# Attention part of a small conv network: full-width products as column-tile pairs, and a new instruction order

## The reference

```
layer 0: q = Wq x + bq (8 x N)   k = Wk x + bk (8 x N)   v = Wv x + bv (32 x N)
         attn = softmax(q^T k)   out = Wo (v attn^T) + bo   x1 = gamma * out + x
layer 1: same with v 64 x N and no Wo:               x2 = x1 + v attn^T
layer 2: batch norm, relu, 3x3 conv with sign weights, twice, plus shortcut
layer 3: per-channel 4x4 whitening over the whole batch (cholesky), 4x4 mix, bias
```

## Time and profile before

| | us |
|---|---|
| median of 3 runs | 70.65 (70.19 to 70.87) |
| profiled execution, its own time | 70.66 |
| its span, first to last instruction | 68.9 |

### The profile page before, as it was taken

One profiled execution on the slowest core, in us unless ns is written; L12 is line 12 of the kernel. 1 busy time (PEld: TensorE's weight loads), 2 busy tenths in 40 slices (PEclk: granted clock), 3 DMA queues, 4 the chain that ended last, 5 costly groups with the idle time before them and its releaser, 6 DMA issues.

```text
span 68.9 us, 1828 instructions
## 1 busy us (share of the span) xinstructions
PE 58.2 (85%) x654; PEld 34.6 (50%) x654; DVE 47.4 (69%) x129; ACT 43.0 (62%) x133; POOL 21.9 (32%) x59
## 2 busy tenths in 40 slices
PE   5997866839999899989695899979998999999910
PEld 2253531416364364445261457358974998774300
DVE  0029799487796987878699754677949969377440
ACT  0710498939989898989999593464008672455440
POOL 4001606860371817355303317470004050008200
PEclk9999999999999999999999999999999999999999
DMA  0889830000000000000000000000000000000025
GB/s 0 237 255 275 274 149 6 0 0 0 0 0 0 10 5 0 0 0 5 0 0 0 5 10 0 0 0 10 0 0 0 0 10 10 0 0 0 0 102 202
DMA packets 2168, 2.69 MB, mean 39 GB/s; under 512 B 368, under 2 KB 1520, under 8 KB 2160
## 3 DMA queue, kind: packets, MB, share of 16 engines
q1 hardware_dynamic: 1872, 2.39, 10.9%
q10 hardware_dynamic: 288, 0.20, 0.9%
HBM read 2.06 MB, written 0.52 MB: 37 GB/s over the span
## 4 chain that ended last, share of the span: by engine, by line
PE 54%; ACT 12%; DVE 11%; POOL 11%; issue 5%; POOLq 1%; DVEq 0%; ACTq 0%
PE bank L760 13%; PE bank L690 9%; ACT bank L458 8%; PE bank L590 6%; PE bank L600 5%; PE bank L624 4%; DVE cut L908 4%; PE bank L735 3%; PE bank L671 3%; POOL zn L405 2%; PE bank L656 2%; PE bank L661 2%; POOL cut L355 2%; POOL cut L358 2%; ACT hi L523 2%
## 5 line engine op out<-in xcount | busy, mean ns | idle before, releaser
L458 ACT ACTIVATE bank<-bank,negmax 128x256 f32<-128x256 f32 x32 | 14.3, 447 | 1.2 <-DVE negmax L898 1.0
L590 PE MATMUL bank<-const-bfloat16-1.0 128*128 128x512 bf16 x39 | 11.2, 419 | 0.8 <-PEq L1177 0.8
L898 DVE TENSOR_REDUCE negmax<-bank 128x2 f32<-128x512 f32 x16 | 10.4, 684 | 1.3 <-PE bank L640 1.3
L471 ACT ACTIVATE probs<-bank 128x512 f32<-128x512 f32 x16 | 8.6, 590 | 0.5 <-PE bank L661 0.5
L690 PE MATMUL bank<-probs,vt 128*64 128x256 f32 x64 | 8.7, 391 | 0.0
L908 DVE TENSOR_SCALAR cut<-bank,prm 128x256 f32<-128x256 f32 x8 | 3.9, 482 | 6.2 <-PE bank L600 6.1
L760 PE MATMUL bank<-hi,taps 64*64 64x225 f16 (+2 forms) x144 | 7.3, 267 | 0.8 <-ACT hi L523 0.8
L760 PE MATMUL bank<-lo,taps 64*64 64x225 f16 (+2 forms) x144 | 7.0, 265 | 0.0
L760 PEld LDWEIGHTS bank<-hi,taps 64*64 64x64 bf16 x144 | 6.0, 107 | 1.9 <-issue 0.9
L458 ACT ACTIVATION_READ_ACCUMULATOR bank<-bank,negmax 128x1 f32 x32 | 6.6, 205 | 0.0
L590 PEld LDWEIGHTS bank<-const-bfloat16-1.0 128*128 128x128 bf16 x39 | 3.9, 108 | 5.2 <-issue 2.5
(11 more groups left out here) (132 smaller groups left out, 101.6 us busy)
## 6 DMA issues: line engine op xcount, KB each, us to landing
cw<-conv_w SPq DMA_DIRECT2D x2, 288.0 KB, 4.6
x<-x_in SPq DMA_DIRECT2D x4, 128.0 KB, 2.7
out<-res SPq DMA_DIRECT2D x2, 256.0 KB, 2.1
kst<-consts SPq DMA_DIRECT2D x1, 428.0 KB, 5.6
aw<-attn_w ACTq DMA_DIRECT2D x1, 128.0 KB, 2.4
aw<-attn_w SPq DMA_DIRECT2D x1, 128.0 KB, 3.2
half<-select SPq DMA_DIRECT2D x1, 96.0 KB, 2.7
kst<-consts SPq DMA_DIRECT2D x1, 64.5 KB, 2.9
```

The costliest lines, as they stand in the source:

```text
L458: nc.scalar.activation(part, part, ACT.Exp, bias=negmax[:, i % 2, n:n + 1], accum_out=total[:, i % 2, n:n + 1]).then_inc(total_out, 1)
L471: nc.scalar.activation(probs[:, i % 2, g], pb_t[g][:].rearrange("p (t n) -> p t n", t=CH), ACT.Exp).then_inc(exp_out, 1)
L590: mm(bank[:], filler, filled, start=True, stop=True)
L898: ve.tensor_reduce(negmax[:, i % 2, g * CH:(g + 1) * CH], pb_s[(2 * i + g) % 3][:].rearrange("p (t n) -> p t n", t=CH), AX.X, ALU.max, neg ...
```

## The change

Three things. First, in the attention part every product with 128 outputs is issued as two with 64 outputs each (column tiles 0 to 63 and 64 to 127): project, replicate, values, shifts_to_rows, the fillers and the identity product of item 7. The products of batch norm and whitening stay as they are; `value_weights` stays too. Second, the order of all four engines' programs is written out call by call instead of in loops. `scores_t(i)` is split into the score products and `add_shifts(i)`; `totals` can be issued by halves, with its Ln as `logs(i)`; `later_parts` of POOL becomes `parts1` and `parts2`. shifts(0) no longer has to follow the later parts of item 1 by its wait, but stands behind those of items 1 and 2 by order; those of item 3 follow it. Signs stay behind the last exps, as they were; weight_sum(1) goes to the end of the attention part, weight_sum(0) and both power_of_two to its late middle. Third, some banks move: `pb_e` to bank 0 (so value_weights waits for qk_out of item 2 and replicate(3) for const0), `proj(3)` to `pb_v`. Fillers: (6, 1, 2) at the start become (6, 1, 5, 4), the two near the end go.

```diff
-WARM_START = (6, 1, 2)
-WARM_ATTENTION = (1, 1, 4, 2)
+WARM_START = (6, 1, 5, 4)
-        pb_e = banks[5]
+        pb_e = banks[0]
-            return (banks[7] if i in (1, 3) else pb_pv)[:, N:2 * N]
+            return {1: banks[7], 3: pb_v}.get(i, pb_pv)[:, N:2 * N]
...
 keep_warm
-                    mm(bank[:], filler, filled, start=True, stop=True)
+                    for h in range(2):
+                        mm(bank[lanes(h)], filler[:, lanes(h)], filled, start=True, stop=True)
 project
-                mm(proj(i), aw[:, w:w + P], x_of(i), start=True, stop=True).then_inc(proj_mm, 1)
+                for h in range(2):
+                    last = mm(proj(i)[lanes(h)], aw[:, w + h * C:w + (h + 1) * C], x_of(i), start=True, stop=True)
+                last.then_inc(proj_mm, 1)
 replicate
+                if i == 3:
+                    pe.wait_ge(const0_set, 1)
                 for o in range(2):
-                    last = mm(pb_rep[:, o * N:(o + 1) * N], half[:, 1 + o, :], tops(cut[:, i]), start=True, stop=True)
+                    for h in range(2):
+                        last = mm(pb_rep[lanes(h), o * N:(o + 1) * N], half[:, 1 + o, lanes(h)], tops(cut[:, i]),
+                                  start=True, stop=True)
 values
-                    last = mm(pb_v[:, t * P:(t + 1) * P], x_of(i)[:, t * P:(t + 1) * P], wv,
-                              start=True, stop=True)
+                    for h in range(2):
+                        cols = t * P + h * C
+                        last = mm(pb_v[lanes(h), t * P:(t + 1) * P], x_of(i)[:, cols:cols + C], wv,
+                                  start=True, stop=True)
 shifts_to_rows
-                    last = mm(pb_rows[:, u * P:(u + 1) * P], tops[:, u, 1::2], half[:, 0, :], start=True, stop=True)
+                    for h in range(2):
+                        last = mm(pb_rows[lanes(h), u * P:(u + 1) * P], tops[:, u, P * h + 1:P * (h + 1):2],
+                                  half[:, 0, :], start=True, stop=True)
```

More of the change, by code:

```diff
@@ L378, in _ @@
             pool.wait_ge(ones16_set, 1)
-            later_parts(1)
+            pool.wait_ge(part2_out, 1)
+            parts1(1)
+            parts2(1)
+            pool.wait_ge(part2_out, 2)
+            parts1(2)
+            parts2(2)
+            pool.wait_ge(part2_out, 3)
             shifts(0)
             pool.wait_ge(shift_out, 1)
[L382 to L388, removed]
+            parts1(3)
+            parts2(3)
+            pool.wait_ge(part2_out, 4)
+            shifts(1)
+            pool.wait_ge(shift_out, 2)
+            shifts(2)
+            pool.wait_ge(shift_out, 3)
+            parts1(4)
+            parts2(4)
+            pool.wait_ge(part2_out, 5)
+            shifts(3)
+            pool.wait_ge(shift_out, 4)
+            parts1(5)
+            parts2(5)
+            pool.wait_ge(part2_out, 6)
+            parts1(6)
+            parts2(6)
+            pool.wait_ge(part2_out, 7)
+            shifts(4)
+            pool.wait_ge(shift_out, 5)
             pool.wait_ge(prm_in, 16)
@@ L454, in totals @@
                 act.wait_ge(max_out, 2 * i + g + 1)
-                for t in range(CH):
+                for t in halves:
                     n = g * CH + t
@@ new lines, in _ @@
+            scores(0)
+            scores_t(0)
+            replicate(1)
+            pe.wait_ge(part0_out, 3)
+            keep_warm(WARM_START[2], pb_pv)
+            scores(1)
+            replicate(2)
+            keep_warm(WARM_START[3], pb_pv)
+            shifts_to_rows(0, 0)
+            value_weights()
+            scores(2)
+            add_shifts(0)
+            values(0, 1)
+            replicate(3)
+            values(1, 1)
+            mix(0)
+            shifts_to_rows(1, 2)
+            scores_t(1)
@@ new lines, in _ @@
+            scores(3)
+            add_shifts(1)
+            project(4)
+            values(2, 2)
+            scores_t(2)
+            shifts_to_rows(2, 3)
+            mix(1)
+            replicate(4)
+            add_shifts(2)
+            project(5)
+            values(3, 3)
+            scores(4)
+            scores_t(3)
+            shifts_to_rows(3, 4)
+            mix(2)
+            replicate(5)
+            add_shifts(3)
+            project(6)
+            scores(5)
+            mix(3)
@@ new lines, in _ @@
+            values(4, 4)
+            replicate(6)
+            project(7)
+            shifts_to_rows(4, 5)
+            scores_t(4)
+            scores(6)
+            add_shifts(4)
+            values(5, 5)
+            shifts_to_rows(5, 6)
+            replicate(7)
+            scores_t(5)
+            add_shifts(5)
+            scores(7)
+            mix(4)
+            shifts_to_rows(6, 6)
+            scores_t(6)
+            add_shifts(6)
+            values(6, 7)
+            mix(5)
+            shifts_to_rows(7, 7)
@@ L732, in combine @@
+            scores_t(7)
+            add_shifts(7)
+            values(7, 8)
+            mix(6)
+            mix(7)
             def combine(n, some):
@@ L955, in _ @@
             queries_keys(0)
+            first_parts(2)
             maxima(0, 0)
```

217 lines of the change are left out of this document (133 added, 84 removed).

## The result

The changed kernel takes 70.17 us (median of 20 runs, 69.94 to 71.99), the kernel before 70.77 beside it (20 runs). The ratio is 0.9938, 95% interval 0.9919 to 0.9957: 0.6% or 0.4 us faster, within the 1% that was set as no change. The forecast was 69.5, a gain of 1.15, and the time lies inside its range of 68.3 to 70.9. Its direction holds, its size doesn't.

A forecast was written before the change was run, and what follows sets the result against it. ACT was taken as the steady loop's bound, with 0.25 us visible idle an item. Start gains 0.65, Ln(7) is 1.1 early, mix(7) 1.25 early; 1.15 taken off gives span 67.75, time 69.5 us, range 68.3 to 70.9.

The forecast's parts named there:

- A tie: Attention's end: shifts_to_rows(7) waits equally for DVE's values_out(6), until 36.75, and POOL's last shift, 36.8; DVE delay counts fully.
- the walk: Step-by-step timing of the new order from measured durations and offsets, start to last mix; gain 1.25 us, 1.15 taken.
- maxima(7,1) is just in time: Late attention loop: DVE's maxima(7,1) doesn't delay ACT's totals(7,0), from 33.35; Ln(7) at 35.75 against 36.84.
- project(2) goes ahead of replicate(0) ... free: Start, on PE: project(2) fits the time in which PE waits for the parts, at no cost.
- On the loop's ring it is worth nothing by itself.: Loop of Ln, POOL, PE, ACT: pairs save 0.35 to 0.4 us of PE an item, but PE waits for POOL.
- Passed through unchanged: Batch norm, convolutions and whitening behind 41.95 keep their time, since the change doesn't touch them.
- 3.1 to the end of mix(7): PE's end after add_shifts(7): values(7) adds 0.6, filler's 0.32 and about 0.1 form change go; mix(7) at 40.7.
- ACT's ledger: Check from exps(0) to exps(7): 21.7 us of work, idle falling from 4.3 to 2.5; 1.25 gained after a 0.5 late start.
- the 0.05 that a half-wide load was to save: PE's change back from 64-row products exposes a load half as wide: 0.05 less.
- the bound of 0.46 an item: Slow 64-wide loads in replicate and shifts_to_rows cost at most 0.46 us an item if none is hidden; near zero taken.
- Rival (b): Order gives little: waits of replicate(3), shifts_to_rows(3), shifts_to_rows(7) each 0.3 longer, as exposed loads would make them; 70.4, chance 0.26.
- Rival (c): Mid-attention ACT stalls of 0.7 and 0.5 don't occur, PE being earlier than walked: another 1.2 off, 68.3, chance 0.10.

The follow-up runs named there:

- swap_power: The changed kernel with values_out(6) put ahead of power_of_two(1) on DVE; 69.78 us, ratio 0.9861.
- order_repaired: The changed kernel with the values_out(6)/power_of_two(1) exchange, project(2) and project(3) moved back later, and all products full-width; 70.33 us, ratio 0.9954.
- order_only: The changed kernel with its pairs turned back into full-width products, new order kept; 71.10 us, ratio 1.0025.
- hybrid: Pairs with the changed kernel's new order up to mix(1) and Ln(3), then the old order of all four engines; 70.42 us, ratio 0.9941.
- pairs_again: The kernel before with pairs only, old order and filler counts, run a second time; 70.94 us, ratio 0.9985.
- same_tile: The changed kernel with both halves of every filler pair put in one column tile; 77.08 us, one execution.
- middle_rows: The changed kernel with shifts_to_rows(3) ahead of scores_t(3) and values(3), and values_out(3) behind maxima(4,1); 70.76 us, ratio 1.003.
- start_and_swap: The changed kernel with values_out(6) ahead of power_of_two(1), project(2) back behind replicate(0) and project(3) behind scores_t(0); 69.48 us, ratio 0.9832.
- pairs_warm: The kernel before with pairs in its old order and four more fillers ahead of 15 us; 70.20 us, ratio 0.9921.
- best_of: The changed kernel with the values_out(6)/power_of_two(1) exchange, shifts_to_rows(3) moved ahead of values(3), and full-width fillers behind attention; 70.08 us, ratio 0.9909.

## Why the prediction was right in direction and wrong in size

**The step that failed** is that of the end: "to 36.35; behind them values_out(6) until 36.75 ... A tie: their cover is used up exactly, and DVE later by d costs d." d was 0.56: values_out(6) ended at 37.31, and shifts_to_rows(7) came 0.55 later than walked, at 37.42 instead of 36.87 (the walk's shift_rows(7), 37.2, less the 0.34 that lies between the two in the trace). The mechanism was named, its queue too; I walked DVE too early. maxima(7) stands in front of these steps. It ended at 33.89, not at the 33.35 from which 36.35 follows, for its row says that it waited 0.55 for scores(7):

```profile
30.90 0.42 PE L697 MATMUL bank<-cut,half 128*64 128x256 bf16 x4 [0.17 <-POOL cut L361]
...
32.60 1.29 DVE L1031 TENSOR_REDUCE negmax<-bank 128x2 f32<-128x512 f32 x2 [0.55 <-PE bank L727]
```

Upward from there: scores(7) waits for qk(7), this for replicate(7) (30.90), and that for POOL's parts(7), which end at 30.84. These stand behind shifts(5), which waited 0.41 for Ln(5), itself 0.26 later than walked; that accounts for about half of the 0.54, and the rest isn't traced. The walk had given "maxima(7,1) is just in time" no error of its own. swap_power shows what it cost: 0.59 from Ln(0) to the first product on all x, and order_repaired has it without pairs, 0.53 (31.11 against 31.64 in order_only, by the chains).

**The start.** "project(2) goes ahead of replicate(0) ... free" was wrong by 0.2 in this profile. PE had only the time up to 6.10 there (replicate(0) in the kernel before), and the project lasts until 6.2. exps(0) is at 13.85 instead of 13.75. What it costs differs by execution, with the landing of x and the clock of the first products: qk(0) waited 0.23 for PE in the profile after, 0.55 in swap_power's, and shows no wait in those of order_only and hybrid. Where PE isn't late the repair gives nothing: Ln(0) is at 10.22 in order_only and at 10.21 in order_repaired, and the difference of their profiles up to the product on all x is the swap's.

**"On the loop's ring it is worth nothing by itself."** Wrong too: pairs alone give some 0.6 us where the clock stays up (ratios 0.9908, and 0.9921 with the fillers). The trace of pairs_again has it, behind its fall, at two places: 0.31 from Ln(3) to Ln(7) (14.75 against 15.06), some 0.08 an item, by scores and project on PE, and 0.23 from exps(7) to the first product on all x (2.48 against 2.71). A row that names POOL as the last to come doesn't say that PE is free of the ring elsewhere.

**Passed through unchanged** was off by 0.17 (above).

**The last stretch came right by luck.** "3.1 to the end of mix(7)" doesn't follow from its own terms: 3.19 + 0.6 - 0.32 - 0.1 is 3.37. It measured 3.18, since the two mixes are shorter by 0.27 together (0.91 and 0.86 for 1.02 each), where the sum had 0.1 of form change.

The account, on the profiled executions: 1.25 walked, 0.10 taken off, 0.40 measured (70.66 less 70.26). Of the missing 0.75, 0.68 lies at exps(7) (38.68 for 38.0), 0.55 of it in the one wait, and 0.17 in the tail, less the 0.10 already taken off. In ACT's ledger exps(0) to exps(7) took 24.83, which is 3.1 of idle over the same 21.7 of work, where the walk had 2.5.

**What held.** A pair costs what one product does (same_tile; project 0.65 as x4 against 0.64 as x2), and the loader's idle before values is gone where it stands behind mix. On the loads, the Trainium skill ("TensorEngine Tiling (Array Packing)", Restrictions) says that column tiling disables Fast Weight Load. The 64-wide 16-bit loads of shifts_to_rows took 108 ns each against 98 for a 128-wide one, which agrees, and speaks against the 0.05 that a half-wide load was to save. They were hidden: four products took 0.42 where two took 0.39 in replicate, so nothing of the bound of 0.46 an item showed. Milestones: Ln(2) 17.20 for 17.15, Ln(3) 20.52 for 20.65, exps(3) 24.63 for 24.35, Ln(5) 28.26 for 28.0, Ln(7) 35.66 for 35.75; ACT's hole of 1.24 at the start is gone, and its stall at 22.66 is there, 0.85 for about 0.7. Rival (b) came nearest in time (70.4) and by its third wait, but not by its reason: no exposed loads. Of its other two waits shifts_to_rows(3) ran about as walked (ACT idle until 22.66 for 22.55), and replicate(3) came 0.28 late (14.03 for 13.75) without moving Ln(2) by more than 0.05. Rival (c) didn't occur, and in middle_rows closing its stall gave nothing.

Why order_only gives nothing, though its Ln(7) is at 35.69: after DVE's wait its add_shifts(7) is at 38.16, 0.60 ahead of the earlier trace rows, and from there it needs 3.70 us to the product on all x where the kernel before needs 3.19: values(7) now stands in that stretch (0.64), a filler of 0.32 is gone, and the identity product takes 0.63 for 0.43. With pairs the same stretch takes 3.18.

What stays open: of the 0.69 us between the change and start_and_swap, the swap is about 0.6 by the traces. What is left for the start isn't shown by times: swap_power (0.9861) and start_and_swap (0.9832) ran in different sets, and their intervals overlap.

## What to carry to other kernels

When work is reordered, write down for every tie of the walk which queues meet there and how late each can be; a tie between an engine that was walked through six items and one that follows from a single wait has to be priced as a loss, and the cheapest mend is to put the step that others wait for first in its queue. Pairs of column tiles kept one form throughout at no cost in PE's time here, but they should stop where the neighbours are full width. A step moved out of a queue needs a place where nothing waits behind it: moved behind values_out(7), power_of_two made DVE the last engine. A stall that a profile shows inside a rearranged loop is only worth closing if the milestones behind it, not just the next one, move. And milestones should be counted from the same event (here Ln(0)), since Ln(0) itself lies between 10.16 and 10.96 us even in the undisturbed profiles.

## What the hardware showed that I had not expected

The granted clock can fall in a kernel whose profile shows it at full speed. The kernel before is one: of its 91 executions beside the later experiments 21 had a mean clock of 0.975 or less and took 70.91 to 73.52 us, where its median in the first set is 70.77. With pairs in the old order it was 6 of 16, low for 3.4 us in one profile and for 6.8 us in the other. Of these six, those with a mean clock of about 0.973 took some 0.9 us longer, those with 0.951 some 2.1, both more than the change gains. In all three profiles with such a fall PE had been busy 2.09 to 2.19 of the 3.70 us ahead of it, near 12 and 14 us with pairs in the old order and ahead of 38.6 us in hybrid.

Of the 32 executions of the changed kernel none had a mean clock under 0.990, and none of the 63 of its variants other than hybrid had one under 0.989, order_only and order_repaired, without pairs, among them. In its own profile (0.990) the clock is low from 67.1 us on only, behind the last product. PE is busy 2.97 of the 3.75 us from 11.5 on there, where the kernel before has 2.15. So the change has a second effect, which the ratios hardly show: falls of this kind didn't occur with it. Whether its order does that or its additional fillers was not run apart; pairs_warm, with fillers alone, speaks for the fillers.

ACT starts its next operation 0.23 us after shift_rows(3) at one place of the new order, and the row calls this "issue" (23.27, above), though the maxima that it needs were done at about 22.85. At the same step of the kernel before the next operation starts right behind the copy (23.56). The gap is there, 0.22 to 0.27 long, in every profile that keeps this stretch of the new order; in middle_rows, best_of and hybrid, which change it, the row there names DVE. Its cause was not settled.
